# A mask ring of five buffers, one NF4 stream through attention steps and FFN units, and x loaded from ScalarE's queue

## The reference

```python
x = x + xattn(layernorm(x), ctx, ctx, mask, Wq, Wk, Wv, Wo)
x = x + ffn(layernorm(x), w1, w2, w3)

# xattn: 32 query heads, 8 key/value heads, 128 wide, rope on q and k
logits = 30 * tanh((q . k) * 0.0884 / 30);  masked;  softmax;  weights . v;  @ Wo

# ffn: w1, w2 (1376 x 512), w3 (512 x 1376), each first quantised to NF4 and back,
# in blocks of 64: idx = searchsorted(bounds, w / absmax); w = CODE[idx] * absmax
h = silu(x @ w1.T) * (x @ w2.T);  out = h @ w3.T
```

## Time and profile before

| | |
|---|---|
| median of 3 runs | 916.22 us (914.02 to 917.31) |
| the profiled execution: its own time | 916.73 us |
| the profiled execution: span | 914.8 us |
| PE busy | 818.3 us, 89% |
| DVE busy | 669.7 us, 73% |
| ACT busy | 466.7 us, 51% |
| POOL busy | 446.3 us, 49% |
| mean DMA rate | 100 GB/s |
| granted TensorE clock, mean | 0.96 |

### The profile page before, as it was taken

One profiled execution on the slowest core, in us unless ns is written; L12 is line 12 of the kernel. 1 busy time (PEld: TensorE's weight loads), 2 busy tenths in 40 slices (PEclk: granted clock), 3 DMA queues, 4 the chain that ended last, 5 costly groups with the idle time before them and its releaser, 6 DMA issues.

```text
span 914.8 us, 10681 instructions
## 1 busy us (share of the span) xinstructions
PE 818.3 (89%) x3806; PEld 650.5 (71%) x3806; DVE 669.7 (73%) x743; ACT 466.7 (51%) x571; POOL 446.3 (49%) x272
## 2 busy tenths in 40 slices
PE   6688893999999999999998998997779797994998
PEld 4576782677788777777886776775567686883886
DVE  3777752788888898888887987888766589698120
ACT  4014742565565656555655655655332576677100
POOL 1645056556857758659659568474102223253000
PEclk9899997999999999999999999999799999998999
DMA  9564735333433423435325234213013013120210
GB/s 328 151 188 140 209 92 169 90 81 93 144 92 90 126 79 114 123 81 155 81 70 167 58 92 144 57 48 101 1 32 133 24 35 114 32 76 23 84 58 35
DMA packets 63540, 91.75 MB, mean 100 GB/s; under 512 B 6784, under 2 KB 30464, under 8 KB 63488
## 3 DMA queue, kind: packets, MB, share of 16 engines
q1 hardware_dynamic: 63488, 91.07, 34.1%
HBM read 51.00 MB, written 19.07 MB: 77 GB/s over the span
## 4 chain that ended last, share of the span: by engine, by line
PE 51%; POOL 15%; DVE 13%; DMA 8%; issue 6%; ACT 5%; SPq 2%; POOLq 0%; DVEq 0%; ACTq 0%
POOL qT L1149 6%; PE bank L463 5%; PE bank L465 4%; PE bank L464 4%; DMA sw<-cs_loop 4%; PE bank L558 4%; PE bank L497 3%; PE bank L499 3%; PE bank L498 3%; PE bank L481 3%; PE bank L482 3%; PE bank L483 3%; PE avp L569 3%; DMA sw<-cs_start 3%; PE trp L470 2%
## 5 line engine op out<-in xcount | busy, mean ns | idle before, releaser
L1149 POOL TENSOR_TENSOR qT<-cs_loop,sw 128x512 f32<-128x512 f32 x58 | 92.6, 1597 | 104.9 <-DMA sw<-cs_loop 99.8
L763 ACT ACTIVATE eb<-bank 128x512 f32<-128x512 f32 x64 | 38.3, 598 | 194.4 <-PE bank L558 194.4
L890 DVE SCALAR_TENSOR_TENSOR nfa<-nfp,nfa 128x1408 f32<-128x1408 uint8 x56 | 106.8, 1907 | 32.5 <-ACT nfp L702 31.2
L890 DVE SCALAR_TENSOR_TENSOR nfv<-nfp,nfv 128x1408 f32<-128x1408 uint8 x56 | 106.5, 1902 | 28.0 <-ACT nfp L702 26.8
L1215 POOL TENSOR_TENSOR eb<-eb,maskf 128x512 f32<-128x512 f32 x64 | 91.1, 1425 | 62.4 <-ACT eb L765 62.4
L702 ACT ACTIVATE nfp<-nfv,bnd 128x1408 uint8<-128x1408 f32 x75 | 107.0, 1460 | 20.4 <-POOL nfv L1165 15.8
L497 PE MATMUL bank<-woh,ath 128*128 128x512 f32 x256 | 109.4, 427 | 0.0
L481 PE MATMUL bank<-xh,wqh 128*128 128x512 f32 x256 | 106.5, 416 | 0.0
L499 PE MATMUL bank<-woh,atl 128*128 128x512 f32 x256 | 103.2, 403 | 0.0
L498 PE MATMUL bank<-wol,ath 128*128 128x512 f32 x256 | 103.0, 402 | 0.0
L890 DVE SCALAR_TENSOR_TENSOR nfx<-nfp,nfx 128x1408 f32<-128x1408 uint8 x42 | 79.9, 1902 | 30.2 <-ACT nfp L702 30.2
(11 more groups left out here) (134 smaller groups left out, 1814.4 us busy)
## 6 DMA issues: line engine op xcount, KB each, us to landing
sw<-cs_loop SPq DMA_DIRECT2D x116, 128.0 KB, 2.3
stage<-wq_pieces SPq DMA_DIRECT2D x32, 256.0 KB, 2.9
stage<-wo_pieces SPq DMA_DIRECT2D x32, 256.0 KB, 2.9
stage<-dq_scratch SPq DMA_DIRECT2D x32, 256.0 KB, 3.2
sw<-cs_start SPq DMA_DIRECT2D x44, 128.0 KB, 2.4
ks_scratch<-qT SPq DMA_DIRECT2D x16, 256.0 KB, 2.3
vs_scratch<-vst SPq DMA_DIRECT2D x16, 256.0 KB, 3.3
kcur<-ks_scratch SPq DMA_DIRECT2D x16, 256.0 KB, 3.2
```

The lines of the kernel that those rows point to most:

```text
L890: op = nc.vector.scalar_tensor_tensor(acc[:, :], nfp[:, n % 2, :], STEPS[i], acc[:, :], ALU.mult, ALU.add)
L1149: nc.gpsimd.tensor_tensor(dst, products(ru, slot)[:, 0, :], sw[:, slot, :], ALU.add).then_inc(roped, 1)
```

## The change

- Chunks 1 to 11 become one stream of 176 positions, 16 for each chunk (15 adds and one empty place). `nf_before(slot)` says how many are done when a slot begins; a slot is an attention step (0 to 63), an FFN unit (64 to 85) or one of two steps of the down stage's weights. It is 116 positions over the 54 steps from 2 to 55, then 1 or 2 a step in head 7, then 2 a unit. A chunk so takes 7.45 steps, and its seams move from head to head.
- The signs of chunks 1 to 10 go into a ring `nfq` of five buffers, one slot ahead of the adds; sign n waits for add n - 5.
- DVE's preparation of a chunk and POOL's normalisation come two steps ahead of its first add, POOL's rescaling one step behind its last add, SP's store one step behind that, its next load another step behind. POOL normalises after the rope of the step, and SP stores and loads after the swap of the step.
- Chunk 0 goes with V units 3 to 13, its signs one unit ahead; its store stands behind the loop over v, and the load of chunk 1 behind v = 13.
- x and chunk 0 are loaded from ACT's queue, x after the tenth high part, chunk 0 after the sixteenth.
- POOL masks step 0 before the sixth query rope and step 1 after it, and normalises chunk 1 in step 0. PE does the logits of step 0 ahead of the sixth query unit. Two low parts (pieces 12 and 14) move from POOL to DVE.
- Chunk 9 gets a buffer of its own, is loaded in head 7, prepared in step 62, and starts with FFN unit 0. The store of chunk 9 moves from the load of weight tile 15 to tile 16. The last three adds of chunk 11 stand behind the first low parts of w3.

The diff, cut to its core:

```diff
+            nfw = sb("nfw", [128, CH], f32, ffn)
+            nfq = sb("nfq", [128, 5, CH], u8, loop)
-        FIRST_POOL = (0, 3, 6, 8, 10, 12, 14, 16, 18, 20, 22, 24, 26)
+        FIRST_POOL = (0, 3, 6, 8, 10, 16, 18, 20, 22, 24, 26)
...
-            return range(15 * v // 13, 15 * (v + 1) // 13) if v < 13 else range(0)
+            return range(15 * (v - 3) // 11, 15 * (v - 2) // 11) if 3 <= v < 14 else range(0)
...
+        def nf_before(slot):
+            if slot <= 56:
+                return max(0, slot - 2) * 116 // 54
+            if slot <= NSTEP:
+                return 116 + (0, 1, 2, 3, 4, 6, 8, 10, 12)[slot - 56]
+            return min(128 + 2 * (slot - NSTEP), 16 * 11)
+        def nf_adds(slot):
+            at = range(nf_before(slot), nf_before(slot + 1))
+            return [(1 + p // 16, p % 16 - p % 16 // 13) for p in at if p % 16 != 12]
+        def nf_prepares(slot):
+            return [c for c in range(2, 12) if nf_before(slot) <= 16 * c - 20 < nf_before(slot + 1)]
+        def nf_finished(slot):
+            return [c for c in range(1, 12) if nf_before(slot) < 16 * c <= nf_before(slot + 1)]
+        def nf_signs(slot):
+            return [(c, i) for c, i in nf_adds(slot + 1) if c < 11] + [(c, i) for c, i in nf_adds(slot) if c == 11]
+        def nf_mask(c, i):
+            n = 15 * c + i
+            return nfq[:, n % 5, :] if 0 < c < 11 else nfp[:, n % 2, :]
...
@@ SP @@
-            sp.dma_start(y[:, :, :], x_d.rearrange("b s d -> s b d")).then_inc(x_in, 16)
-            nf_load(0)
...
-                if v == 13:
+                if v == 14:
                     nf_load(1)
-                if v == 14:
-                    nf_store(0)
...
+            nf_store(0)
...
+                    query_swap(j + AHEAD)
...
+                    for c in nf_finished(j - 2):
+                        nf_store(c)
+                    for c in nf_finished(j - 3):
+                        if c < NKV - 1:
+                            nf_load(c + 2)
+                    if last and b == 2:
+                        sp.wait_ge(proj_done, NK + NUNIT)
+                        nf_load(NKV + 1)
...
-                if n == 15:
+                if n == 16:
                     nf_store(NKV + 1)
...
@@ PE @@
+                    if v == 15:
+                        logits(0)
                     q_unit(u)
...
@@ ACT @@
-                wait(act, nf_acc, n - 1)
-                nc.scalar.activation(nfp[:, n % 2, :], nf_bufs(c)[0][:, :], ACT.Sign, bias=bnd[:, i:i + 1])\
+                wait(act, nf_acc, n - 4 if 0 < c < 11 else n - 1)
+                nc.scalar.activation(nf_mask(c, i), nf_bufs(c)[0][:, :], ACT.Sign, bias=bnd[:, i:i + 1])\
...
             for n in range(16):
                 first_hi(n)
+                if n == 9:
+                    act.dma_start(y[:, :, :], x_d.rearrange("b s d -> s b d")).then_inc(x_in, 16)
+            act.dma_start(nfv[:, :], nf_d[:, 0:CH]).then_inc(nf_in, 16)
...
-                for i in nf_values(v):
+                for i in nf_values(v + 1):
                     nf_above_bound(0, i)
...
-                    bounds = nf_head(kv, b)
+                    signs = nf_signs(j)
...
@@ DVE @@
-                    bounds = nf_head(kv, b)
-                    before = max(1, len(bounds) - 1)
+                    adds = nf_adds(j)
+                    before = max(1, len(adds) - 1)
...
-                    if b == 6 and not last:
-                        nf_prepare(kv + 2)
+                    for c in nf_prepares(j):
+                        nf_prepare(c)
...
+                if 1 <= n < 3:
+                    for c, i in nf_adds(NSTEP + 2 * HT + n - 1):
+                        nf_add(c, i)
...
@@ POOL @@
             for u in range(AHEAD):
+                if u == 5:
+                    mask(0)
                 query_rope(u)
...
-            nf_normalise(1)
+            mask(1)
...
-                    if b == 7 and not last:
-                        nf_normalise(kv + 2)
-                    if b == 0 and kv > 0:
-                        nf_rescale(kv)
+                    for c in nf_finished(j - 1):
+                        nf_rescale(c)
...
+                    for c in nf_prepares(j) if j else (1,):
+                        nf_normalise(c)
```

More of the change, by code:

```diff
@@ L115, in build @@
         atl = sb("atl", [128, 4, 512], f32r)
+        with ExitStack() as loop:
+            nfq = sb("nfq", [128, 5, CH], u8, loop)
         vst = sb("vst", [128, 4, 512])
@@ L534, in _, with logits @@
                     first_transposes(u - 10)
+            def logits(j):
+                kv, h, s = j // B, j % B // 4, j % 4
+                if s == 0:
+                    pe.wait_ge(roped, NK + 8 * kv + 4 * h + 4)
+                    pe.wait_ge(k_in[h], 16 * kv + 16)
+                wait(pe, tanh_done, j)
+                nc.tensor.matmul(lgp[:, :], kcur[:, h, s * 128:(s + 1) * 128],
+                                 qT[:, h, :, s * 128:(s + 1) * 128], start=True, stop=True).then_inc(logits_done, 1)
             for v in range(16):
@@ L770, in head @@
                     j = 8 * kv + b
-                    bounds = nf_head(kv, b)
-                    for i in bounds[0:1]:
-                        nf_above_bound(kv + 1, i)
+                    signs = nf_signs(j)
+                    for c, i in signs[0:1]:
+                        nf_above_bound(c, i)
                     if not last:
@@ L780, in head @@
                     nc.scalar.activation(ath[:, j % 4, :], trp[:, :], ACT.Copy).then_inc(at_hi, 1)
-                    for i in bounds[1:]:
-                        nf_above_bound(kv + 1, i)
+                    for c, i in signs[1:]:
+                        nf_above_bound(c, i)
                     if last and b == 5:
@@ L1033, in head @@
                         ALU.mult).then_inc(an_done, 1)
[L1035 to L1040 removed]
+                    adds = nf_adds(j)
+                    before = max(1, len(adds) - 1)
+                    for c, i in adds[:before]:
+                        nf_add(c, i)
+                    for c in nf_prepares(j):
+                        nf_prepare(c)
                     u = j + AHEAD
@@ L1043, in head @@
                         rope_parts(NK + u, u % 2, csq[:, :, :])
-                    for i in bounds[before:]:
-                        nf_add(kv + 1, i)
+                    for c, i in adds[before:]:
+                        nf_add(c, i)
+                    if j == 0:
+                        nf_prepare(1)
                     dve.wait_ge(at_hi, j + 1)
@@ L1238, in head @@
                         power(2, range(2, 4))
-            mask(0)
-            mask(1)
             for kv in range(NKV):
```

140 lines of the change are left out of this document (53 added, 87 removed).

## The result

The changed kernel takes **888.09 us** (median of 4 runs, 886.71 to 888.37) beside 915.12 us before (4 runs, 911.23 to 917.31): a ratio of 0.971, interval 0.967 to 0.974. The number of rival A was 879.

The account below looks back on a forecast made before the run. PE, busy 89%, was taken as bound by idle stretches, mostly behind NF4 work, and low clock after them. Gains 7.5 + 4.0 + 14.4 + 9.8 + 8.1 + 17.0 = 60.8 from 916.7 gave 856 us, range 844 to 880.

Parts of the forecast that it names:

- rival A: Steps 3 to 57: DVE adds and POOL operations never run together, 93% bookable, loop 446 us, total 879; chance 0.16.
- The start: K units: first swap no longer queues behind x and chunk 0, PE's 5.60 us stand goes; gain 7.5 (5 to 8.1).
- rival B: Start, loop entry, loop, head 7: queues only move the wait, gains at lower bounds or half, 871 us; chance 0.11.
- rival B's sign: POOL's wait for a swap again over 5 us in the start, or ropes as PE's releaser.
- V units: V units: signs start at unit 2, so PE's waits for V copies go; gain 4.0 (2 to 5).
- Into the loop: Before step 0: store behind swaps, masks earlier, chunk 1's normalisation later; gain 14.4 (11 to 15.5).
- Steps 3 to 57: Attention loop: 14.8 us lost at head seams, reordering leaves 5 of them; gain 9.8 (0 to 13).
- The signs that A was to show: Loop: adds over 2.1 us in the mean, POOL's 128x512 operations near 2, steps over 7.9 throughout.
- Head 7: Head 7: only 1 or 2 adds a step, so late `nrm` and rope waits shrink; gain 8.1 (4 to 9).
- FFN units: FFN: chunk 9 ready in head 7, its store no longer holds tile 15; gains 4.7 and 6.3.
- Down stage: Before the down stage: five adds ahead of w3's first low part become two; gain 5.9.

Follow-up runs that it names:

- experiment 7: Changed kernel with x issued after ACT's sixteenth high part: 887.06 us; with x as eight 256 KB loads behind the first four ropes: 888.53 us.
- Experiment 8: Changed kernel, chunk 1 prepared before step 0, normalised behind the second mask: 882.55 us; also three head weight pieces issued before chunk 0's store: 879.97 us.
- experiment 4: Kernel before the change, adds of chunks 1 to 8 after each first replaced by equally long one-input reductions: 898.72 us.
- Experiment 9: Changed kernel with chunk 11's last signs and adds moved behind the high and low parts of w3's tiles 1 and 2: 876.26 us.
- experiment 10: Changed kernel with entry edit, early weight pieces, and signs and adds from the last FFN unit on behind w3's tiles: 866.26 us, again 866.93.
- experiment 6: Changed kernel with the weight pieces' low parts in heads 0 to 6 moved from POOL to DVE: 898.59 us.
- experiment 3: Changed kernel, adds of chunks 1 to 8 after each first replaced by equally long one-input reductions on DVE: 863.08 us.
- experiment 1: Changed kernel with chunks 2 to 8 prepared and normalised one step earlier: 883.88 us.

## Why the prediction was wrong, step by step

**The start, 4.1 for 7.5, under the lower bound.** The swap left the queue in time (13.25) and then shared the engines with x and the pieces: 7.7 us. The forecast took nearly the whole gain, as if the swap did not wait, without a row for it; 5 was the end that the sharing gives. POOL stands 9.5 us for the first swap, which was rival B's sign. The Trainium skill ("DMA: Bandwidth & Descriptors", Issuing engines are not separate DMA queues) had spoken against this part, and experiment 7 agrees with it in its numbers: 3 us for a swap with nothing fresh ahead, 7.7 and over 8 behind x.

**V units, 3.9 for 4.0**: right, PE's waits for V copies are gone from the list.

**Into the loop, 11.3 for 14.4.** Right until step 0, which starts 23 us earlier. Then "the old steps 1 and 2 lost as much, so I count that at nothing" failed: step 2 took 13.4 us. The forecast saw ACT's first sign wait for chunk 1 and priced it at 1 to 3 us; ACT stood 6.63, and 7.19 more for a piece that SP now issues behind its store and its waits. Experiment 8 gets 3.8 and 0.5 us of it back. Here and in the start rival B (5 and 11) was nearer than the forecast.

**Steps 3 to 57, -11.9 for +9.8: the step that failed.** Two sentences of it were wrong. "14.8 us are lost there, at the seams of heads": the seams were where the loss showed, not what made it alone (experiment 4: 418.0 us with the old order, once the adds no longer exclude POOL). And "so 7.09 of 7.74. It fits" counted DVE by itself. The sum to make was that of rival A. I take the lengths that operations have alone: 1.61 us for an add with two inputs, 0.91 for a chunk's first add, 1.29 and 2.55 on POOL. The change: 101 x 1.61 + 7 x 0.91 + 162 x 1.29 + 14 x 2.55 = 414 of 441.0 to 444.7 us, 93 to 94%. Before, with 94 adds of two inputs, 402 of 432.8, 93%. Old pace in new order, with 96 + 6 adds and 12 long operations, 400 of 428.7, 93%. Three programs stop at the same share, rival A's 93%; why not at more no run shows. (A booked all adds at 1.61, one add too many, and POOL at 1.26; these nearly cancel.) Its 446 us for the loop came within 1.3 of 444.7 and 5 of 441.0; its 879 for the whole was 9 short, since it had the forecast's gains everywhere else. Its chance of 0.16 was too low. The argument against it ("in the undisturbed steps it is 7.0 of 7.74 already, and PE waits for nothing") looked at a step in which all met well. The Trainium skill ("SBUF — State Buffer", SBUF: two separate sides) describes this as an exclusive lock for the whole instruction, between GpSimd and a DVE operation that has two SBUF inputs or runs in a 2-port perf mode. The trace agrees for two inputs: add and low part each end about their own length after the other. The first add with its one input lengthened a rescaling from 2.55 to 3.2 us; whether it ran in such a mode no run here shows.

**The signs that A was to show** were only half right: low parts at 2.3, masks at 1.76, but adds at 1.97 in the mean of the loop, not over 2.1, and 44 of the 54 steps still within 0.15 of 7.74. Nearly all of the loss comes in seven steps of 8.9 to 14.7 us. Six of them are steps whose logits need the last of four ropes: POOL falls behind, and PE pays when that rope is late.

**Head 7, 9.0 for 8.1; FFN units, 13.1 for 11.0**: right in mechanism and size. Chunk 9 and tile 15 no longer wait.

**Down stage, -1.3 for +5.9.** The forecast counted five adds becoming two before the first low part, and that came: the stand fell from 11.74 to 5.68 us. It did not follow the three adds that now stand before tiles 1 and 2: PE stands 4.2 us more at tile 2 and is busy 3.1 us longer (69.2 for 66.1) at a lower clock (0.91 for 0.93 over the stage). Moved adds cost where they arrive. Experiment 9 won 6.1 us of the stage, and experiment 10 in all 11.6, with the clock at 0.99 (10.0 and 0.97 in its second run).

## What to carry to other kernels

Before more work goes on two engines that may exclude each other, add up their operations at the lengths they have alone, both engines in one sum; here no more than 94% of the stretch could be booked. Then add up the one engine with what it is held (experiment 6). A mean well over the shortest duration of the same shape (1.91 beside 1.61) was that exclusion at work, not jitter, and replacing the operation by one of equal length that does not lengthen the other's tells it from a full engine. When a wait vanishes from the list, ask what its engine does now: in the loop before, adds stood 61.7 us for signs, and for 46.3 of these POOL was at work undisturbed.

## What the runs showed of the hardware that I had not expected

- In the loop, 101 adds with two inputs and 175 POOL operations made POOL 102 us and DVE 37 us busier than the same program with reductions (344.1 and 390.2 beside 242.5 and 353.6). Reductions of 1408 columns to 22, with one input, left POOL's 128x512 operations at means of 1.29 to 1.30 us and its normalisations at 2.55.
- An operation with one input can hold POOL as well: beside a chunk's first add (128x1408, 0.91 us) rescalings took 3.2 us and not 2.55, in seven of seven chunks of experiment 4.
- Waits of 5.6 to 7.0 us on ACT in front of tanh, 24.1 us in all, cost PE 1.5 us while POOL and DVE were in time (experiment 3), and removing them won nothing while they were late (experiment 1).
- A swap (two transfers of 128 KB) reached POOL in 3 us when a 2 MB load was issued 2.6 us behind it, in 7.7 when the load was issued 1.7 us ahead, and in over 8 when it was issued 4 us ahead with chunk 0's right behind it.
- The same code gave 441.0 and 444.7 us for the same 54 steps, and 134.9 to 136.5 us for the start of step 0, in different executions.
